# Quantised activations turned by DMA transpositions instead of TensorE transposes, with unrolled steps

## The reference, cut to what matters

```python
def act_quant(x):
    scale = 127.0 / jnp.clip(jnp.max(jnp.abs(x), axis=-1, keepdims=True), 1e-05)
    q = jnp.clip(jnp.round(x * scale), -128.0, 127.0) / scale
    return x + jax.lax.stop_gradient(q - x)
def bitlinear(x, w, b):
    xq = act_quant(rmsnorm(x))
    wq = weight_quant(w)
    return jnp.einsum('bsd,fd->bsf', xq, wq) + b
h = bitlinear(x, w1, b1)
h = jax.nn.gelu(h, approximate=False)
return bitlinear(h, w2, b2)
```

## Time and profile before

| | us |
|---|---|
| median of 3 runs | 1394.94 (1390.99 to 1401.05) |
| profiled execution: span from first to last instruction | 1396.9 |
| TensorE busy, whole span | 1241.2 (89%) |
| VectorE, ScalarE, GpSimd busy | 1011.6, 855.6, 528.6 |
| stretch 0 to 265 (preparing, steps 0 and 1): TensorE busy | 154.42 |
| stretch 925.70 to 998.30 (one loop step): TensorE busy | 71.88 of 72.60 |
| the same stretch: VectorE, ScalarE, GpSimd busy | 55.70, 49.06, 27.83 |
| stretch 1284.90 to 1396.90 (steps 16 and 17): TensorE busy | 82.37 of 112.00 |

### The profile page before, as it was taken

How to read it: one execution, slowest core, us unless ns; L and a number is a source line. 1 busy time by engine, 2 the same in 40 slices (tenths; PEclk the granted TensorE clock), 3 DMA queues, 4 the chain that set the end, 5 groups by cost and what they waited for, 6 DMA issues and landing times.

```text
span 1396.9 us, 24632 instructions
## 1 busy us (share of the span) xinstructions
PE 1241.2 (89%) x8500; PEld 816.6 (58%) x8788; DVE 1011.6 (72%) x2102; ACT 855.6 (61%) x1613; POOL 528.6 (38%) x484
## 2 busy tenths in 40 slices
PE   4635757899999999999999899999999999999875
PEld 3423533666666666667575657576766666665532
DVE  3698546887777778786869586878787777776654
ACT  1284554475858585757575575857575858585534
POOL 1244368543425151616161434343343425152320
PEclk9755677999999999999999999999999999999987
DMA  8246533102010111110110202020202011100000
GB/s 298 94 166 222 192 99 116 56 10 71 18 62 24 60 26 60 26 60 15 72 49 16 79 15 72 15 71 0 77 9 69 17 62 24 46 16 31 0 16 16
DMA packets 51853, 85.59 MB, mean 61 GB/s; under 512 B 5456, under 2 KB 23376, under 8 KB 50128
## 3 DMA queue, kind: packets, MB, share of 16 engines
q1 hardware_dynamic: 49504, 82.59, 18.0%
q10 hardware_dynamic: 2304, 2.40, 0.6%
HBM read 57.97 MB, written 9.18 MB: 48 GB/s over the span
## 4 chain that ended last, share of the span: by engine, by line
issue 34%; DVE 22%; ACT 18%; POOL 12%; PE 11%; DMA 2%; SPq 1%; POOLq 0%; DVEq 0%; ACTq 0%
ACT e L713 6%; DVE h L1233 4%; POOL rs L502 3%; POOL hid L511 3%; POOL r L523 2%; ACT rl L745 2%; ACT h L774 2%; PE ps L1583 2%; ACT q L778 2%; POOL e L506 2%; ACT sq L756 2%; DVE r L943 2%; PE ps L1493 2%; PE ps L1506 1%; DVE qS L1083 1%
## 5 line engine op out<-in xcount | busy, mean ns | idle before, releaser
L502 POOL TENSOR_TENSOR rs<-ve,nhalf 128x1 f32<-128x1 f32 x160 | 96.1, 601 | 604.6 <-DVE ve L1075 432.6
L1493 PE MATMUL ps<-xT,fcT 128*128 128x256 f16 x2048 | 260.6, 275 | 0.0
L1506 PE MATMUL ps<-pjT,hid 128*128 128x512 fp8e4 x1024 | 241.8, 385 | 2.2 <-POOL hid L511 2.2
L1493 PEld LDWEIGHTS ps<-xT,fcT 128*128 128x128 fp8e4 x2048 | 202.3, 99 | 26.5
L511 POOL TENSOR_TENSOR hid<-sq,hid 128x512 f16<-128x512 f32 x128 | 157.4, 1235 | 22.1 <-ACT sq L756 14.5
L1506 PEld LDWEIGHTS ps<-pjT,hid 128*128 128x128 f16 x1024 | 96.3, 99 | 97.9 <-issue 6.0
L745 ACT ACTIVATE rl<-ps,rsf 128x256 f32<-128x256 f32 x256 | 107.8, 477 | 43.7 <-PE ps L1493 43.7
L713 ACT ACTIVATE e<-ps,nmb,sig 128x128 f32<-128x128 f32 x256 | 113.5, 461 | 27.5 <-DVE nmb L1119 27.5
L1583 PE MATMUL ps<-w2T,hT 128*128 128x512 fp8e4 x512 | 117.5, 383 | 5.8 <-ACT hT L790 5.8
L1558 PE MATMUL ps<-w1T,q4T 128*128 128x512 fp8e4 x512 | 120.4, 385 | 0.0
L783 ACT ACTIVATE q<-h 128x2048 f16<-128x2048 f32 x32 | 61.2, 1911 | 96.6 <-DVE h L1244 96.6
(11 more groups left out here) (209 smaller groups left out, 2436.2 us busy)
## 6 DMA issues: line engine op xcount, KB each, us to landing
h<-in_w SPq DMA_DIRECT2D x12, 1024.0 KB, 5.2
xb<-in_x SPq DMA_DIRECT2D x16, 512.0 KB, 3.5
qS<-qT SPq DMA_DIRECT2D x128, 64.0 KB, 2.0
r1b<-r SPq DMA_DIRECT2D x16, 512.0 KB, 3.0
out<-r SPq DMA_DIRECT2D x32, 256.0 KB, 2.5
xa<-in_x SPq DMA_DIRECT2D x15, 512.0 KB, 3.7
rope<-in_rope SPq DMA_DIRECT2D x16, 384.0 KB, 3.2
hid<-in_w SPq DMA_DIRECT2D x4, 1024.0 KB, 6.3
```

Of the source, the lines that this page charges most:

```text
L502: pool.tensor_tensor(rs[:, n, t:t + 1], ve[:, n, t:t + 1], nhalf[:, :], ALU.pow).then_inc(done, 1)
L1493: mm = pe.matmul(dst, fcT[:, k, f * P:(f + 1) * P], xT2[:, xs, k, :], start=False, stop=(xs == 1 and k == KC - 1))
L1506: mm = pe.matmul(ps[:, FFN0 + t, :], hid[:, xs, c, t * P:(t + 1) * P], pjT[:, c, :], start=(c == 0 and xs == 0), stop=(c == FC - 1 and xs ...
```

## The change

The TensorE transposes `t4` and `t5` and the ScalarE copies `t4_out` and `t5_out` are gone. SyncE's queue issues a DMA transposition per tile from `q4` into `q4T` and from `q5` into `hT`, which now holds both tiles. The consumers wait for the DMA's semaphores, the back part's banks are renumbered (14 uses a group instead of 20), and SyncE's order is new. All steps are straight code on every engine. The slots of what stays are as they were. The size of a DMA scratch area is set too.

```diff
-        hT = sb("hT", [P, FC, P], F16)
+        hT = sb("hT", [P, TILES, FC, P], F16)
...
-            low=(120,), t3=(193, 201), wx=(203, 211), t4=(211, 223), w1=(223, 223, 226, 226, 230, 230, 235, 235),
-            t5=(239, 247), w2=(245, 250))
+            low=(120,), t3=(193, 201), wx=(203, 211), w1=(223, 223, 226, 226, 230, 230, 235, 235), w2=(245, 250))
...
         def main_loop(eng, body, change_at=None, change=None):
...
+            for j in range(GROUPS + STAGES - 1):
+                if change is not None and j == change_at:
+                    change()
                 body(j)
...
+            def turn_q4(g, t):
+                need(sp, q4_done, 2 * TILES, g, 2 * t + 1)
+                sp.dma_start_transpose(q4T[:, :, t * P:(t + 1) * P], q4[:, t, :]).then_inc(q4T_in[t], 16)
+
+            def turn_q5(g, t):
+                need(sp, q5_done, TILES, g, t)
+                sp.dma_start_transpose(hT[:, t, :, :], q5[:, :]).then_inc(hT_in[t], 16)
...
                 if ga is not None:
                     pair_heads(ga)
+                if gb is not None:
+                    for t in range(TILES):
+                        turn_q4(gb, t)
...
                 if ga is not None and more:
                     next_rope(ga)
+                if gb is not None:
+                    turn_q5(gb, 0)
+                if ga is not None and more:
                     next_xb(ga)
+                if gb is not None:
+                    turn_q5(gb, 1)
+                    store(gb, 0)
                 if ga is not None:
                     keep_r1(ga, gf)
                 if gb is not None:
-                    for t in range(TILES):
...
+                    store(gb, 1)
...
             def gelus(g, t):
                 need(act, h_done, 4 * TILES, g, 4 * t + 3)
                 act.activation(h[:, t, :], h[:, t, :], ACT.Gelu).then_inc(gelu, 1)
-                if not (first(g) and t == 0):
-                    act.wait_ge(t5_ps, g * (2 * TILES) + 2 * t)
+                if t > 0:
+                    act.wait_ge(hT_in[t - 1], g * 16 + 16)
+                elif not first(g):
+                    act.wait_ge(hT_in[TILES - 1], g * 16)
                 need(act, gelu, TILES, g, t)
...
             def w1_up(g, t, n):
                 u = 4 * t + n
-                if u == 0:
+                if u == 1:
+                    need(pe, x3_done, TILES, g, 0)
+                elif u == 2:
                     need(pe, x3_done, TILES, g, 1)
-                    need(pe, q4T_done, TILES, g, 0)
-                elif u == 2:
-                    need(pe, q4T_done, TILES, g, 1)
                 elif u >= 3:
                     need(pe, h_done, 4 * TILES, g, u - 3)
-                    if u == 4:
-                        need(pe, q4T_done, TILES, g, 1)
+                if n == 0:
+                    pe.wait_ge(q4T_in[t], g * 16 + 16)
...
             def w2_down(g, t):
-                if t == 0:
-                    need(pe, h_done, 4 * TILES, g, 7)
-                else:
-                    need(pe, out_done, TILES, g, 0)
-                need(pe, hT_done, 2 * TILES, g, 2 * t + 1)
-                pe.ldweights(hT[:, 0, :], tile_position=(0, 0))
+                pe.wait_ge(hT_in[t], g * 16 + 16)
+                pe.ldweights(hT[:, t, 0, :], tile_position=(0, 0))
...
-    nc = bacc.Bacc("TRN2", target_bir_lowering=False, num_devices=1)
+    nc = bacc.Bacc("TRN2", target_bir_lowering=False, num_devices=1,
+                   dynamic_dma_scratch_size=1024)
```

More of the change, by code:

```diff
@@ L216, in build @@
         out_stored = [sem(f"out_stored{t}") for t in range(TILES)]
+        q4T_in = [sem(f"q4T_in{t}") for t in range(TILES)]
+        hT_in = [sem(f"hT_in{t}") for t in range(TILES)]
         (ln1, rs1, xn1, t1_ps, x1hi, x1lo, q_ps, rot_mul, rot_sum, q_hi, q_lo, s_ps, s_max, s_bias, s_exp, s_inv,
@@ L226, in build @@
             "up_ps relu sq_done hid_hi hid_lo down_ps down_mul x2_done").split()]
[L228 to L231, removed]
+        (ln3, rs3, xn3, t3_ps, x3hi, x3lo, x2c, wx_ps, x3_done, ln4, rs4, z4, q4_done, x3b, w1_ps,
+         h_done, gelu, sqsum, z5, rs5, q5_round, q5_done, w2_ps, out_done) = [sem(n) for n in (
+             "ln3 rs3 xn3 t3_ps x3hi x3lo x2c wx_ps x3_done ln4 rs4 z4 q4_done x3b w1_ps "
+             "h_done gelu sqsum z5 rs5 q5_round q5_done w2_ps out_done").split()]
         def need(eng, s, per, g, k):
@@ L251, in build @@
         ON_DVE = 4
+        STAGES = 3
         def here(places, p):
             return [k for k, at in enumerate(places) if at == p]
-        FIRST = 3
         PE_AT = dict(
@@ L468, in _ @@
             body(2, 1, 0)
-            with sp.Fori(3, PER_BATCH - 1) as i:
-                body(i, i - 1, i - 2)
+            for j in range(3, PER_BATCH - 1):
+                body(j, j - 1, j - 2)
             j = PER_BATCH - 1
@@ L477, in _ @@
             body(j + 2, j + 1, j)
-            with sp.Fori(PER_BATCH + 2, GROUPS - 1) as i:
-                body(i, i - 1, i - 2)
+            for j in range(PER_BATCH + 2, GROUPS - 1):
+                body(j, j - 1, j - 2)
             j = GROUPS - 1
@@ L783, in q5_int @@
                 act.activation(q5[:, :], h[:, t, :], ACT.Copy, bias=-MAGIC).then_inc(q5_done, 1)
[L785 to L791, removed]
             def body(j):
@@ L1532, in mix @@
                 mm.then_inc(wx_ps, 1)
[L1534 to L1543, removed]
@@ L1556, in w1_up @@
                 pe.ldweights(q4T[:, 0, t * P:(t + 1) * P], tile_position=(0, 0))
                 for k in range(KC):
-                    mm = pe.matmul(back_bank(6 + u), q4T[:, k, t * P:(t + 1) * P], w1T[:, k, n * 512:(n + 1) * 512],
+                    mm = pe.matmul(back_bank(4 + u), q4T[:, k, t * P:(t + 1) * P], w1T[:, k, n * 512:(n + 1) * 512],
                                    start=(k == 0), stop=(k == KC - 1))
                 mm.then_inc(w1_ps, 1)
[L1562 to L1570, removed]
-                        mm = pe.transpose(back_bank((14, 17)[t] + a).bitcast(F16)[:, c * P:(c + 1) * P], q5[:, f:f + P],
-                                          ident16[:, :])
-                    mm.then_inc(t5_ps, 1)
@@ L1611, in body @@
                         mix(g, t)
-                    for t, g in due(PE_AT["t4"], j, s):
-                        t4(g, t)
                     for n, g in due(PE_AT["w1"], j, s):
@@ L1617, in body @@
                         w2_down(g, t)
-                    for t, g in due(PE_AT["t5"], j, s):
-                        t5(g, t)
                     if isinstance(j, int) and j < 2:
```

37 lines of the change are left out of this document (12 added, 25 removed).

## The result

The changed kernel takes 1401.81 us (median of 14 runs, 1396.56 to 1405.64), the kernel before 1396.57 (14 runs, 1390.99 to 1401.05). The ratio is 1.0038 with a 95% interval of [1.0024, 1.0052]. In size that lies within the 1% that the prediction takes for no change, and within its range, but the interval excludes a gain: the sign of the forecast is wrong.

What follows compares the result with a forecast made beforehand. The prediction took a full TensorE and an equally long circle through VectorE, GpSimd and ScalarE as the bound. Gains of 4.8 (steps) and 1.1 (unrolling) less 0.4 (last step) took 5.5 us off 1394.9: 1389 us, range 1371 to 1418.

Steps and rivals of the forecast that it cites:

- The second circle: From `q_proj` over VectorE, GpSimd, ScalarE to `t2`, then TensorE to the next `q_proj`: a step gains at most 1.37 us.
- `q4` is hidden in the steps: The DMA turn of `q4`, taken as 2.5 us, has 7 us of cover or more in a step: costs nothing.
- SyncE's order: `next_rope`, `next_xb`, `store` 0 and `keep_r1` issue later, behind the turns; their data is wanted tens of us later: nothing.
- The start of the last `w1_up`: In the last step, `w1_up` begins at 1357.3 instead of 1359.95 thanks to the `q4` turn: 2.65 us gained.
- the list of signs: Expected in the changed profile: waits of about 1 us before `w2_down` and 1.5 before `t2`, period near 72.1 us.
- L: Time from the end of `q5_int` to the release of the waiter on the turn of `q5`: taken as 4.2 us.
- The formula: Per step: L beyond the 3.17 us of cover at `w2_down` of tile 1 is paid, 1.37 gained; net 0.34 gained.
- Unrolling: Straight code for 12 loop steps, judged by the already straight step 2: 0.09 us each, 1.1 us gained.
- The fourth rival: Straight code is slower than the loop in all twelve steps, at 1 us a step: 1402 us; chance 0.05.
- Step 16 "at nothing": The step before the last was left without any gain or loss.
- the last step: No other work beside it: `w1_up` gains 2.65, `w2_down` starts 1.28 later and runs 1.8 slower; together 0.4 us lost.
- The sum: Whole kernel: 4.8 us gained in steps 2 to 15, 1.1 from unrolling, 0.4 lost at the end: 5.5 us faster.

Runs made afterwards that it cites:

- experiment one: The kernel before with its loops written out as straight code on every engine, nothing else changed: 1398.28 us, ratio 1.0005.
- experiment four: The changed kernel with `w2_down` of tile 1 moved behind `t1` and its `x4_out` one slot later: 1397.25 us, ratio 0.9994 to the kernel before.
- Experiment eight: Kernel with each `q5` turn split in halves, in loops, but groups 14 and 15 turned by TensorE and ScalarE again: 1375.82 us, against 1382.22 for split turns alone.
- experiments two: The changed kernel with hardware loops again on the four compute engines, SyncE staying straight: 1398.30 us, ratio 1.0004 to the kernel before.
- experiment seven: The changed kernel with a quarter of each `q5` turned a second time before its readers may start: 1475.27 us, ratio 1.0589.

## Why the prediction went wrong, by its steps

**The second circle: right.** I said that at most 1.37 us of the 2.24 that TensorE loses can come out of a step, 0.47 of it by way of `q4`. The turn of `q4` alone gave 0.49, and the split turn, with nothing waiting for `hT`, 1.24. That `q4` is hidden in the steps is right, as is SyncE's order. The start of the last `w1_up` looks right too (1357.3 forecast, 1357.57 found), but that is chance: counted from the last `q_proj` it comes at 142.2 instead of 141.4, and the 0.8 comes out of step 16 (below). In the list of signs I wrote 1.5 us for the wait at `t2`; it is 0.85 to 1.06, and my own numbers would have said so: 0.20 + 1.34 less the 0.47 by which the chain comes earlier is 1.07.

**L: right in kind, mis-sized by 0.18.** "It is one instruction like `r1b`, with work by pieces behind it like `qS`; I take 4.2": it was 4.38. The formula does the rest. 72.54 - 1.37 + (4.38 - 3.17) = 72.38, and the undisturbed steps take 72.34 to 72.38. The term costs 16 x 0.18 = 2.9 us of the forecast gain of 5.5, and 4.38 still lies under the break-even of 4.54, so L alone would not have turned the sign. Of the two rules that I weighed, that of the Trainium skill's "Advanced Engine Details and Errata", section "X-Bar Transpose (TRN2)", by which a transposing DMA is as fast as a regular one, doesn't hold for these 512 KB: 4.3 us against 2.9 for the copy. The Trainium skill's sequencer times in "DMA: Bandwidth & Descriptors", section "Why a DMA increments its semaphore by 16 and not by 1", erred the other way: an estimated 3.4 us for the issuing instruction, where SyncE's rows show 1.3 to 3.0. That the sum by them, 1401, hits the measured 1401.81 is luck: it stands on L = 4.9, and the rest of the loss came from elsewhere.

**Unrolling: the step that failed.** "The unrolled step is a full one, so nothing in it speaks for a loss." I took step 2 of the kernel before as the sample and added 1.1 us of gain. The sample was sound for that kernel, as experiment one shows, but the changed one has a wait for a DMA on its path in every step. The views count the instruction packets on the same 16 DMA engines. In step 3 two of them go with a turn that lands 0.9 us late, and the step is 0.95 us longer; in loops, with 26 packets on q8 instead of 64, that is gone, and with more cover for the same late landing (experiment four) too. So +1.1 was forecast; the traces of the changed kernel and its loops show 2 us the other way, the medians 5. I priced the two edits one by one and never together. The fourth rival had the right subject and the wrong mechanism: it charged every step for its code, where the price is paid in a few steps that wait for a transfer. This step does not carry the sign alone: with loops the kernel still stood at 1.0004, because L, the end and the batch change had taken the rest of the forecast gain.

**Step 16 "at nothing", and the last step: wrong.** Counted from the last `q_proj`, which came 0.55 us earlier than before, the last `w2_down` was to end 0.4 us later than before and ended 2.0 later (1.7 in the second trace of the changed kernel). Of the 1.6 between, 0.9 is step 16: there `w2_down` of tile 1 waits 6.37 us, runs at 0.67 of the clock and ends 0.34 later, though its step began 0.55 earlier. Twice the error in L is 0.36, and 0.38 is that the last run took 5.81 us where I had added 1.8 to 3.63. Experiment eight shows that the turns in these two steps together cost 4 to 7 us in the split version.

**The sum.** In the traces the thirteen intervals came out at +1.05 us. They hold 13 x 0.34 + 12 x 0.09 = 5.5 of the forecast gain, so they miss by 6.6: 2.3 is L, 1.7 the four long steps, 1.6 the step of the batch change, 0.6 the smaller gain from straight code, and 0.4 is left. The part behind them shows +2.0, and the part ahead of them, which the change hardly touches, -1.6; there the first `q_proj` of step 2 starts anywhere from 260.1 to 267.6 in the traces of this case, without a pattern. So the traced spans differ by 1.5 us and the medians by 5.2, which lies within what one trace's head varies by. Of the 5 us that loops recover by the medians, only some 2 have a place in a trace; whether the others are real, and where they are, is open.

What stays open too is why the batch-change step takes 81.89 and 81.56 in the changed kernel against 80.51 before. There `mix` took 5.00 us at 0.52 of the clock (4.70 in the second run of the kernel, 3.30 to 4.59 in the others), with the wait ahead of `scores` at 5.3 to 6.0 us in all of them.

## What to carry to other kernels

When a transfer takes the place of work on the bounding engine, price it by its landing time against the cover of its first reader, and where it doesn't fit, split it so that the reader can start on the first part: that turned 5 us of loss into 13 of gain. A step without neighbouring work pays the transfer in full and, in the traces here, the engine's clock on top (experiment eight), so try the old way in the drain. Straight code that shows no cost in one kernel may have one in another whose path waits for a DMA; measure such a pair of edits together.

## What the runs showed of the hardware, unexpected

- A transposition from SBUF to SBUF of 16-bit data landed 2.5 us after issue for 128 KB, 3.2 for 256 KB and 4.3 for 512 KB; the plain copy of 512 KB took 2.9. Its packets are small: those under 512 bytes went from 5456 to 89424.
- In steps 2 to 15 the same transposition, for tile 1, landed 4.5 to 5.2 us after issue where an instruction packet moved beside it, and after 4.3 elsewhere, in both traces of the changed kernel and those of experiments two and four. That the packet is the cause is read from this and from the two steps that loops repaired; no run moved a packet alone.
- TensorE's clock fell after some waits of 2 to 4 us and not after others of the same length. In experiment seven, after a wait of 2.24 us, `t2` took 1.92 instead of 1.18 and the 16 matmuls behind it 4.51 instead of 3.62; after one of 3.35 us `w2_down` took 3.63 in one step and 5.31 in the next. In all traces here `w2_down` took 4.9 to 6.3 us after the waits of 4.03 to 13.2 us. In this kernel a TensorE that waits longer can also compute more slowly, which made the seventh experiment some 17 us dearer than its waits.
